# Expert numbers packed and read once, routed blocks written out, and 11 of 32 experts loaded beside the blocks

## The chip, the cores and the metric

The kernel runs on one core of a Trainium2 chip. The metric is the device time of the whole program in microseconds. The time before is 4682.44 us, the median of three runs (4677.71 to 4683.45).

## The reference

Two layers work on 1792 tokens (32 sequences of 56) with 256 features. Each has a cross attention and a feed-forward part, each behind a layer norm and added to its input. The change lies in the feed-forward part of layer 0, a mixture of 32 experts (M = 176) beside a shared expert of twice that width:

```python
scores = sigmoid(x @ gate_w)
# two groups of eight experts are masked out, six of the rest are selected
weights = original_scores[selected] / sum
xs = x_exp[argsort(selected)]             # 6 x 1792 rows, sorted by expert
g = ragged_dot(xs, w_gate, group_sizes)
u = ragged_dot(xs, w_up, group_sizes)
d = ragged_dot(silu(g) * u, w_down, group_sizes)
expert_out = sum(d[unsorted] * weights)
shared = silu(x @ sw_gate) * (x @ sw_up) @ sw_down
out = expert_out + shared
```

All of it is float32 in the reference. The kernel computes each such product as three float16 products (high x high, high x low, low x high), weights and rows being kept as a high and a low half.

## The kernel before

Six phases follow one another: queries, attention and mixing of layer 0, its experts, then queries and attention of layer 1, and the last feed-forward part. The phases named here are `mix0_phase` and `experts_phase`.

**The end of mix0_phase.** Routing gives every (token, choice) a row in a buffer in which each expert has a whole number of blocks of 256 rows, at least one; there are NBX = 74 blocks in all, sorted by expert. VectorE counts for each block which expert it belongs to (L1161 to L1163), TensorE turns the column into a row (L1218), and VectorE copies the 74 numbers as int32 into `g.be` (L1165). GpSimd had set the two words ahead of them to zero (L1030).

**experts_phase** has a queue of turns, one per block u. The blocks 0 to 13 are the shared expert, two halves for each of seven blocks of tokens; u = 14 to 87 are the 74 routed blocks. An `up` of a block is 18 matmuls (gate and up projection), a `down` 10; TensorE runs up(u) and then down(u - 2), so that ScalarE, VectorE and GpSimd have two blocks of time for the activation between them.

- SyncE (SP) loads the weights of an expert with five DMAs (`weights`, L1333 to L1337) into one of three staging buffers. During the shared turns it loads in each turn two experts and one tile of 112 token rows (`rows`, L1342). In a routed turn u it issues, in this order, the transposed load of the rows of block u + 2 (`load_x`, L1310, behind up(u)), the weights of an expert if there is one in this turn, and the store of block u - 2 (`store_y`, L1317, behind the copy of its result).
- ScalarE converts an expert's staged weights to the high halves in four operations (L1430 to L1434), and behind that computes the turn's silu (`gate_`, L1441) and the high half of the activation.
- VectorE makes the low halves of the weights in four operations (L1476 to L1483), then the turn's product (L1496) and the copy of the result of block u - 2 out of PSUM (L1518).
- GpSimd scatters the tiles of token rows into the sorted buffer, 96 indirect DMAs (L1392), six for each of 16 tiles, with four buffers for the tiles. Behind that it computes the low half of the activation in every routed turn (L1405).

The routed blocks begin when all 96 sends have landed, since SP waits for them ahead of the first two loads of x. Which experts are loaded in a turn says `experts_at`: 28 of them two by two in the turns 0 to 13, and four in the turns 14 to 17. The turns up to u = 19 and the last ones are written out on SP, ScalarE, VectorE and GpSimd, the rest is a loop over pairs of turns (`blocks`).

TensorE has an order of its own. `group` (L1588) reads ten expert numbers into its registers, eight for the blocks of the group and two more because `down` is two blocks behind, and then runs eight blocks with them. Four groups are written out (the blocks 0 to 31, which wait for the weights of expert t ahead of block t, L1594), five run in a loop, and the last group has two blocks. The numbers in the registers are added to the address of the weights in each matmul.

Of the kernel before, what the change touches and what calls it, by code (L numbers as in the profile page):

```python
# [32 lines left out]
NB = NBX + NBS  # L33
NU = NBX + 2 * NBS
LAG = 2
F = 1024
FB = F // 128
WS = 64.0
# [33 lines left out]
def later(tile, d):  # L72

    n, par, half = tile
    return n + d, (par + d) % 2, half + (par + d) // 2
# [842 lines left out]
def mix0_phase(nc, g, io):  # L918

    with phase(nc) as (ctx, a):  # L920
# [31 lines left out]
        jcol = a.sb("m_jcol", [128, 1])  # L952
        past = a.sb("m_past", [128, NE])
        bcol = a.sb("m_bcol", [128, 1])
        pY = a.ps("m_pY", [128, 512])
        pX = a.ps("m_pX", [128, 512])
        pL = a.ps("m_pL", [128, 512])
# [44 lines left out]
        @block.gpsimd  # L1002
        def _(pool):
            def rstd(t, k, _):
                pool.wait_ge(s["var"], t + 1)
                nc.gpsimd.tensor_tensor(rs[:], ve[:], g.mhalf[0:TT, 0:1], ALU.pow).then_inc(s["rstd"], 1)

            def rows(t, k, half):

                pool.wait_ge(s["xn_ready"], t + 1)  # L1010
                wait(pool, kept[k], 16 * half)
                passed(pool, p_gate)
                row = xn[:, k].rearrange("t (p c) -> t c p", c=KC)
                high, low = (xr[:, k, n].rearrange("t (c p) -> t c p", c=KC) for n in range(2))
                nc.gpsimd.tensor_copy(high, row).then_inc(s["rows"], 1)
                pool.wait_ge(s["rows"], 2 * t + 1)
                passed(pool, p_gate)
                nc.gpsimd.tensor_tensor(low, row, high, ALU.subtract).then_inc(s["rows"], 1)

            made = Counted(pool, s["made"])  # L1020
            made(nc.gpsimd.memset(ones[:], 1.0))
            made(nc.gpsimd.iota(jcol[:], [[0, 1]], base=0, channel_multiplier=1,
                                allow_small_or_imprecise_dtypes=True)).done()

            made(nc.gpsimd.affine_select(out=before[:], in_=ones[:], compare_op=ALU.is_ge, fill=0.0, base=-1,
                                         pattern=[[1, 128]], channel_multiplier=-1))
            for n in range(2):
                made(nc.gpsimd.affine_select(out=spread[:, n], in_=ones[0:NE, 0:NE], compare_op=ALU.is_ge, fill=0.0,
                                             base=n - 1, pattern=[[1, NE]], channel_multiplier=-1))
            made(nc.gpsimd.memset(g.be[:, 0:LAG], 0))  # L1030
            pipeline(pool, NT, [(rstd, 0), (rows, -1)])

        @block.scalar
# [23 lines left out]
        def _(dve):  # L1057
# [99 lines left out]
            own(nc.vector.tensor_copy(g.s6[:], s8[:, :, 0:TOPK]))  # L1157
            own(nc.vector.tensor_scalar(g.idx[:], s8[:, :, 0:TOPK], 1.0, None, ALU.subtract))

            dve.wait_ge(s["made"], 6)  # L1160
            own(nc.vector.tensor_scalar(past[:], pX[:, NE:2 * NE], jcol[:, 0:1], None, ALU.is_le)).done()  # L1161
            own(nc.vector.tensor_reduce(bcol[:], past[:], AX.X, ALU.add)).done()
            nc.vector.tensor_scalar(bcol[:], bcol[:], NE - 1.0, None, ALU.min).then_inc(s["listed"], 1)  # L1163
            dve.wait_ge(s["turned"], 1)
            nc.vector.tensor_copy(g.be[:, LAG:LAG + NBX], pY[0:1, 0:NBX]).then_inc(s["filled"], 1)  # L1165

        @block.tensor
        def _(pe):
# [52 lines left out]
def experts_phase(nc, g, io):  # L1221
# [4 lines left out]
    GB = 8  # L1226
    NSH = 2 * NBS
    STG = 3
    PER = 2
    FIRST = [NE, NE + 1]  # L1230
    LINE = FIRST + list(range(NE))
    AT = {e: n for n, e in enumerate(LINE)}
    LATE = NE - PER * NSH
    SENDS = [(t, k) for t in range(NT) for k in range(TOPK)]
    with phase(nc) as (ctx, a):
        stg = a.sb("d_stg", [128, STG, 2, KC, M])
# [34 lines left out]

        def blocks(eng, turn, high):

            for u in range(-high, NSH + 6):
                turn((u, u % 2, u // 2))
            pairs = (NU - high - NSH - 6) // 2
            with eng.Fori(0, pairs) as i:
                turn((2 * i + NSH + 6, 0, i + NSH // 2 + 3))
                turn((2 * i + NSH + 7, 1, i + NSH // 2 + 3))
            for u in range(NSH + 6 + 2 * pairs, NU + LAG):  # L1280
                turn((u, u % 2, u // 2))

        def main(e, n):
# [11 lines left out]
        def experts_at(u):  # L1295

            if not isinstance(u, int):
                return []
            if u == -1:
                return FIRST  # L1300
            if 0 <= u < NSH:
                return list(range(PER * u, PER * u + PER))
            return [PER * NSH + u - NSH] if NSH <= u < NSH + LATE else []

        def load_x(eng, gate, tile):
            v, vk, _ = tokens_of(tile)
# [231 lines left out]
        def _(pe):  # L1538
            def up(tile, e):
                u, k, _ = tile  # L1540
                _, vk, vhalf = tokens_of(tile)
                pe.wait_ge(x_in[vk], 16 * vhalf + 16)

                wait(pe, s["h_ready"], 2 * (u - 1))
                for n in range(3):
                    out = ps[k][n] if n < 2 else ps[k][n][0:64 + MT]
                    for c in range(KC):
                        last = three_products(nc, out, columns(e, 0, n, c), columns(e, 1, n, c), xb[:, vk, 0, c],
                                              xb[:, vk, 1, c], start=(c == 0), stop=(c == KC - 1))
                last.then_inc(s["up_done"], 1)  # L1550
# [19 lines left out]
            def down_shared(v):  # L1570
# [5 lines left out]
                        last = down_part(pd[v % 2][:, b], k, NE + k, slice(b * 128, (b + 1) * 128), k == 0, k == 1)  # L1576
                last.then_inc(s["down_done"], 2)

            pe.wait_ge(s["zeroed"], 2)
            pe.wait_ge(s["w_lo"], 8)  # L1580
            for u in range(NSH):
# [1 line left out]
                if u > LAG and u % 2:  # L1583
                    down_shared((u - LAG) // 2)

            def group(i, count):

                _, held = nc.values_load_multi_w_load_instructions(  # L1588
                    g.be[0:1, ds(GB * i, count + LAG)], [mybir.EngineType.PE], min_val=0, max_val=NX - 1)
                for n in range(count):  # L1590
                    tile = (GB * i + n + NSH, n % 2, GB // 2 * i + n // 2 + NSH // 2)
                    if isinstance(i, int) and GB * i + n < NE:

                        pe.wait_ge(s["w_lo"], 4 * AT[GB * i + n] + 4)  # L1594
                    up(tile, held[n + LAG])
                    if isinstance(i, int) and GB * i + n < LAG:
                        if n == LAG - 1:
                            down_shared(NBS - 1)
                    else:
                        down(later(tile, -LAG), held[n])  # L1600
                return held[count:]

            full = NBX // GB
            for i in range(NE // GB):
                group(i, GB)
            with pe.Fori(NE // GB, full) as i:
                group(i, GB)
            for n, e in enumerate(group(full, NBX - GB * full)):
                u = NU - LAG + n
                down((u, u % 2, u // 2), e)  # L1610

def q1_phase(nc, g, io):
# [923 lines left out]
def build(nc, io):  # L2537
    with ExitStack() as ctx:
# [16 lines left out]
        io.xs = nc.dram_tensor("scratch_xs", [TOK, H], F32, kind="Internal").ap()  # L2555
        with ExitStack() as inner:
            b = Alloc(nc, inner)
            g.be = b.sb("be", [1, LAG + NBX], I32)
            g.comb = b.sb("comb", [TT, NT, NE])
            g.slot = b.sb("slot", [TT, NT, NE])  # L2560
            g.s6 = b.sb("s6", [TT, NT, TOPK])
            mix0_phase(nc, g, io)
            g.wg = b.sb("wg", [128, NX, 2, 2, KC, 128], F16)
            g.wt = b.sb("wt", [128, NX, 2, KC, 64 + MT], F16)
            g.wd = b.sb("wd", [128, NX, 2, 2, H], F16)
            experts_phase(nc, g, io)
# [41 lines left out]
```

## Time and profile before

| | us |
|---|---|
| median of three runs | 4682.44 |
| lowest and highest run | 4677.71, 4683.45 |
| the profiled execution's own time | 4708.63 |
| its span in the trace | 4706.5 |
| TensorE (PE) busy | 3904.1 (83%) |
| VectorE (DVE) busy | 3443.8 (73%) |
| GpSimd (POOL) busy | 2778.1 (59%) |
| ScalarE (ACT) busy | 2449.9 (52%) |

The rows in this document come from one profiled execution. Times are microseconds from the start of the span; busy time is that of instructions that compute or send; register, branch and semaphore instructions and the issuing of DMAs by SP do not count as busy. In the rows, PEq and SPq are the sequencers of TensorE and SyncE, L12 is line 12 of the kernel, and `out<-in` names what an instruction writes and reads. A helper's matmuls carry the helper's lines (L111 to L113). A bracket at the end of a row is the idle time of the engine before it and what ended it; "issue" is time in which the engine waited for nothing that the profile shows. PEclk is the granted TensorE clock as a share of full speed. The experts phase lies between 2758 and 3216 us.

### The profile page before, as it was taken

The page shows a single profiled execution, that of the slowest core. Times are in us where ns is not written, and L with a number is a line of the kernel's source. Part 1 is how long each engine was busy: PE and PEld are TensorE (multiplying, and loading weights), DVE is VectorE, ACT ScalarE, POOL GpSimd, SP SyncE. Part 2 cuts the span into 40 slices and gives each one's busy share as a digit, 9 for nine tenths or more (in the row PEclk, how much of TensorE's full clock was granted, in tenths as well). Part 3 has the DMA queues.
Part 4 walks back from the last instruction along what each step waited for, and adds up shares of the span by engine and source line. Part 5 has one row for each costly group of instructions (what it writes and reads, how often), then busy time and mean ns, then how long its engine had stood idle before and what let it go on. Part 6 is the DMA issues. An engine that isn't in the chain of part 4 may idle for free. (4 is left out here: it accounts for less than half of the span.)

```text
span 4706.5 us, 104529 instructions
## 1 busy us (share of the span) xinstructions
PE 3904.1 (83%) x34578; PEld 2973.1 (63%) x34579; DVE 3443.8 (73%) x5403; ACT 2449.9 (52%) x4087; POOL 2778.1 (59%) x2145
## 2 busy tenths in 40 slices
PE   5669999999999999999999735883199999999945
PEld 3437777767767776777777724773167767677734
DVE  4657787877877777878877236445789888888957
ACT  4635555545545555555555114331157777777843
POOL 5577777767767776777773144335635555555632
PEclk8879999999999999999999967996599999999966
DMA  6357777767767677687774547554344444444410
GB/s 242 113 133 148 167 153 160 168 132 162 161 141 163 145 159 150 152 173 150 155 160 103 172 127 215 140 141 126 113 123 130 119 123 125 124 118 129 110 38 25
DMA packets 1236097, 657.45 MB, mean 140 GB/s; under 512 B 1087825, under 2 KB 1162449, under 8 KB 1230654
## 3 DMA queue, kind: packets, MB, share of 16 engines
q1 hardware_dynamic: 1218654, 606.60, 54.8%
q0 software_dynamic: 9216, 22.03, 1.6%
q10 hardware_dynamic: 7760, 22.55, 1.3%
q8 instruction: 298, 4.88, 0.4%
q14 instruction: 169, 1.38, 0.1%
HBM read 187.16 MB, written 142.34 MB: 70 GB/s over the span
## 5 line engine op out<-in xcount | busy, mean ns | idle before, releaser
L2007 POOL TENSOR_TENSOR b_pTl<-b_pe,b_pTh 125x1344 f16<-125x1344 f32 x192 | 538.4, 2804 | 482.8 <-ACT b_pTh L2066 458.4
L111 PE MATMUL a_pa<-a_pTh,a_ch 125*128 125x224 f16 x3072 | 796.5, 259 | 1.9 <-DMA a_pTl<-a_pl 1.9
L113 PE MATMUL a_pa<-a_pTh,a_cl 125*128 125x224 f16 x3072 | 795.5, 259 | 0.0
L112 PE MATMUL a_pa<-a_pTl,a_ch 125*128 125x224 f16 x3072 | 795.4, 259 | 0.0
L826 POOL TENSOR_TENSOR a_ksq<-a_kb 125x512 f32<-125x512 f32 x384 | 474.0, 1234 | 350.9 <-DVE a_kb L759 283.4
L698 ACT ACTIVATE a_pr<-a_pr,a_nmax 112x1500 f32<-112x1500 f32 x256 | 395.7, 1546 | 374.3 <-DVE a_nmax L777 374.2
L843 POOL TENSOR_TENSOR a_kb<-a_kb,a_rk 125x512 f32<-125x512 f32 x384 | 540.4, 1407 | 69.1 <-POOL a_kb L843 34.8
L791 DVE SCALAR_TENSOR_TENSOR a_pl<-a_pr,a_inv,a_ph 112x1500 f16<-112x1500 f32 x256 | 502.3, 1962 | 46.1 <-ACT a_ph L705 45.2
L705 ACT ACTIVATE a_ph<-a_pr,a_inv 112x1500 f16<-112x1500 f32 x256 | 395.5, 1545 | 222.1 <-DVE a_inv L786 222.1
L2112 DVE TENSOR_REDUCE b_mx<-b_ps 112x3 f32<-112x1500 f32 x256 | 439.0, 1715 | 95.3 <-PE b_ps L2189 93.9
L777 DVE CUSTOM_DVE_ANT_0 a_pr<-a_ps,a_mask 112x1500 f32<-112x1500 f32 x256 | 438.8, 1714 | 70.3 <-PE a_ps L113 65.3
L2059 ACT ACTIVATE b_pe<-b_pt 125x448 f32<-125x448 f32 x768 | 393.3, 541 | 163.2 <-PE b_pt L2211 157.8
L747 DVE TENSOR_REDUCE a_ssk<-a_ksq 125x8 f32<-125x1024 f32 x192 | 233.9, 1218 | 223.2 <-POOL a_ksq L826 222.5
L111 PE MATMUL a_pw<-a_wk,a_cT 128*128 128x512 f16 x768 | 304.3, 396 | 91.5 <-DVE a_kTl L765 42.7
L688 ACT ACTIVATE a_kTh<-a_pw 128x500 f16<-128x500 f32 x384 | 224.8, 585 | 251.1 <-PE a_pw L869 249.8
L2066 ACT ACTIVATE b_pTh<-b_pe 125x1344 f16<-125x1344 f32 x256 | 337.0, 1317 | 5.0 <-PE b_po L2227 1.8
L837 POOL TENSOR_TENSOR a_rk<-a_rk,mhalf 125x8 f32<-125x8 f32 x192 | 314.2, 1636 | 35.2 <-POOL a_rk L833 35.2
L112 PEld LDWEIGHTS a_pa<-a_pTl,a_ch 125*128 125x128 f16 x3072 | 301.0, 98 | 23.9 <-issue 0.3
L759 DVE SCALAR_TENSOR_TENSOR a_kb<-a_pw,a_bk 125x512 f32<-125x512 f32 x384 | 262.7, 684 | 70.0 <-PE a_pw L113 64.4
L111 PEld LDWEIGHTS a_pa<-a_pTh,a_ch 125*128 125x128 f16 x3072 | 300.3, 98 | 21.3 <-DVE a_al L797 2.1
L765 DVE TENSOR_TENSOR a_kTl<-a_pw,a_kTh 128x500 f16<-128x500 f32 x384 | 256.1, 673 | 69.3 <-ACT a_kTh L688 68.9
L111 PE MATMUL a_ps<-a_kTh,a_qh 128*112 128x500 f16 x768 | 294.3, 383 | 14.1 <-DVE a_nmax L777 13.2
(376 smaller groups left out, 10953.5 us busy)
## 6 DMA issues: line engine op xcount, KB each, us to landing
b_ks<-b_kn SPq DMA_DIRECT2D x768, 93.8 KB
scratch_cT<-a_cT SPq DMA_DIRECT2D x64, 768.0 KB
b_cT<-scratch_cT SPq DMA_DIRECT2D x32, 1536.0 KB
a_ctx<-ctx SPq DMA_DIRECT2D x128, 360.0 KB
scratch_xd<-q_zero ACTq DMA_DIRECT2D x4, 4736.0 KB
scratch_yd<-e_y SPq DMA_DIRECT2D x74, 256.0 KB
scratch_oT<-a_ot SPq DMA_DIRECT2D x16, 896.0 KB, 4.2
m_oT<-scratch_oT SPq DMA_DIRECT2D x16, 896.0 KB
```

What stands on the lines that cost most here:

```text
L111: nc.tensor.matmul(out, a_hi, b_hi, start=start, stop=False)
L112: nc.tensor.matmul(out, a_hi, b_lo, start=False, stop=False)
L113: return nc.tensor.matmul(out, a_lo, b_hi, start=False, stop=stop)
L698: nc.scalar.activation(pr[:, n % 2], pr[:, n % 2], ACT.Exp, scale=-1.0, bias=nmax[:, par, n:n + 1], accum_out=rsum[:, par, n:n + 1]).then_ ...
L705: nc.scalar.activation(ph[:, n % 2, :, 0:KP], pr[:, n % 2].rearrange("p (k c) -> p k c", c=KP), ACT.Copy, scale=inv[:, par, n:n + 1]).then ...
L777: nc.vector.tensor_tensor_reduce(out=pr[:, n % 2].rearrange("p (a k) -> p a k", k=500), in0=ps_s[0:RP, :, 0:500], in1=mask[:].rearrange("p ...
L791: nc.vector.scalar_tensor_tensor(pl[:, n % 2, :, 0:KP], pr[:, n % 2].rearrange("p (k c) -> p k c", c=KP), inv[:, par, n:n + 1], ph[:, n % ...
L826: nc.gpsimd.tensor_tensor(ksq[:, n % 4], kb[0:KP, n % KBN], kb[0:KP, n % KBN], ALU.mult).then_inc(s["k_squared"], 1)
L843: nc.gpsimd.tensor_tensor(k4, k4, rk[:, 1, NKV * t:NKV * t + NKV].unsqueeze(2) .to_broadcast([KP, NKV, HD]), ALU.mult).then_inc(s["k_norme ...
L2007: nc.gpsimd.tensor_tensor(pTl[:, n % 2, :, 0:RP], pe_[:, n % NP], pTh[:, n % 2, :, 0:RP], ALU.subtract).then_inc(s["l_pool"], 1)
L2059: nc.scalar.activation(pe_[:, r % NP, 4 * third:4 * third + 4], ps_t[at % 2][0:KP, 0:4 * RP].rearrange("p (k c) -> p k c", c=RP), ACT.Exp) ...
L2112: nc.vector.tensor_reduce(mx[:, par, n], ps_s[0:RP, :, 0:500], AX.X, ALU.max).then_inc(s["max_ready"], 1)
```

## The change

The 74 expert numbers are packed four to a word, as digits to the base 32, into 19 words. TensorE reads the 19 words into registers once, ahead of the shared blocks, and takes each number out of its word with a division and a remainder where it is first used. All 74 routed blocks are written out on TensorE; the groups and their loop are gone. 21 experts are loaded in the turns 0 to 13 (alternately one and two), and 11 in every second turn from 14 to 34. The turns up to u = 35 are written out on the other engines (`LONG` = 36). In `mix0_phase` VectorE multiplies the 76 entries by 1, 32, 1024 and 32768 and adds them by fours, two operations ahead of the copy; GpSimd makes the four factors in four memsets instead of one memset of `g.be`.

```diff
@@ -33,6 +33,8 @@
 NB = NBX + NBS
 NU = NBX + 2 * NBS
 LAG = 2
+PACK = 4
+NWORD = -(-NBX // PACK)
 F = 1024
 FB = F // 128
 WS = 64.0
@@ -952,6 +954,9 @@
         jcol = a.sb("m_jcol", [128, 1])
         past = a.sb("m_past", [128, NE])
         bcol = a.sb("m_bcol", [128, 1])
+        digit = a.sb("m_digit", [1, PACK])
+        digits = a.sb("m_digits", [1, NWORD, PACK])
+        word = a.sb("m_word", [1, NWORD])
         pY = a.ps("m_pY", [128, 512])
         pX = a.ps("m_pX", [128, 512])
         pL = a.ps("m_pL", [128, 512])
@@ -1027,7 +1032,8 @@
             for n in range(2):
                 made(nc.gpsimd.affine_select(out=spread[:, n], in_=ones[0:NE, 0:NE], compare_op=ALU.is_ge, fill=0.0,
                                              base=n - 1, pattern=[[1, NE]], channel_multiplier=-1))
-            made(nc.gpsimd.memset(g.be[:, 0:LAG], 0))
+            for n in range(PACK):
+                made(nc.gpsimd.memset(digit[:, n:n + 1], float(NE ** n)))
             pipeline(pool, NT, [(rstd, 0), (rows, -1)])
 
         @block.scalar
@@ -1157,12 +1163,15 @@
             own(nc.vector.tensor_copy(g.s6[:], s8[:, :, 0:TOPK]))
             own(nc.vector.tensor_scalar(g.idx[:], s8[:, :, 0:TOPK], 1.0, None, ALU.subtract))
 
-            dve.wait_ge(s["made"], 6)
+            dve.wait_ge(s["made"], 5 + PACK)
             own(nc.vector.tensor_scalar(past[:], pX[:, NE:2 * NE], jcol[:, 0:1], None, ALU.is_le)).done()
             own(nc.vector.tensor_reduce(bcol[:], past[:], AX.X, ALU.add)).done()
             nc.vector.tensor_scalar(bcol[:], bcol[:], NE - 1.0, None, ALU.min).then_inc(s["listed"], 1)
             dve.wait_ge(s["turned"], 1)
-            nc.vector.tensor_copy(g.be[:, LAG:LAG + NBX], pY[0:1, 0:NBX]).then_inc(s["filled"], 1)
+            own(nc.vector.tensor_tensor(digits[:], pY[0:1, 0:NWORD * PACK].rearrange("a (w n) -> a w n", n=PACK),
+                                        digit[:].unsqueeze(1).to_broadcast([1, NWORD, PACK]), ALU.mult)).done()
+            own(nc.vector.tensor_reduce(word[:], digits[:], AX.X, ALU.add)).done()
+            nc.vector.tensor_copy(g.be[:], word[:]).then_inc(s["filled"], 1)
 
         @block.tensor
         def _(pe):
@@ -1226,11 +1235,11 @@
     GB = 8
     NSH = 2 * NBS
     STG = 3
-    PER = 2
+    EARLY = 21
+    LONG = NSH + 2 * (NE - EARLY)
     FIRST = [NE, NE + 1]
     LINE = FIRST + list(range(NE))
     AT = {e: n for n, e in enumerate(LINE)}
-    LATE = NE - PER * NSH
     SENDS = [(t, k) for t in range(NT) for k in range(TOPK)]
     with phase(nc) as (ctx, a):
         stg = a.sb("d_stg", [128, STG, 2, KC, M])
@@ -1271,13 +1280,13 @@
 
         def blocks(eng, turn, high):
 
-            for u in range(-high, NSH + 6):
+            for u in range(-high, LONG):
                 turn((u, u % 2, u // 2))
-            pairs = (NU - high - NSH - 6) // 2
+            pairs = (NU - high - LONG) // 2
             with eng.Fori(0, pairs) as i:
-                turn((2 * i + NSH + 6, 0, i + NSH // 2 + 3))
-                turn((2 * i + NSH + 7, 1, i + NSH // 2 + 3))
-            for u in range(NSH + 6 + 2 * pairs, NU + LAG):
+                turn((2 * i + LONG, 0, i + LONG // 2))
+                turn((2 * i + LONG + 1, 1, i + LONG // 2))
+            for u in range(LONG + 2 * pairs, NU + LAG):
                 turn((u, u % 2, u // 2))
 
         def main(e, n):
@@ -1299,8 +1308,9 @@
             if u == -1:
                 return FIRST
             if 0 <= u < NSH:
-                return list(range(PER * u, PER * u + PER))
-            return [PER * NSH + u - NSH] if NSH <= u < NSH + LATE else []
+                return list(range(EARLY * u // NSH, EARLY * (u + 1) // NSH))
+            n = EARLY + (u - NSH) // 2
+            return [n] if u >= NSH and u % 2 == 0 and n < NE else []
 
         def load_x(eng, gate, tile):
             v, vk, _ = tokens_of(tile)
@@ -1576,6 +1586,8 @@
                         last = down_part(pd[v % 2][:, b], k, NE + k, slice(b * 128, (b + 1) * 128), k == 0, k == 1)
                 last.then_inc(s["down_done"], 2)
 
+            _, words = nc.values_load_multi_w_load_instructions(
+                g.be[0:1, 0:NWORD], [mybir.EngineType.PE], min_val=0, max_val=NE ** PACK - 1)
             pe.wait_ge(s["zeroed"], 2)
             pe.wait_ge(s["w_lo"], 8)
             for u in range(NSH):
@@ -1583,31 +1595,28 @@
                 if u > LAG and u % 2:
                     down_shared((u - LAG) // 2)
 
-            def group(i, count):
-
-                _, held = nc.values_load_multi_w_load_instructions(
-                    g.be[0:1, ds(GB * i, count + LAG)], [mybir.EngineType.PE], min_val=0, max_val=NX - 1)
-                for n in range(count):
-                    tile = (GB * i + n + NSH, n % 2, GB // 2 * i + n // 2 + NSH // 2)
-                    if isinstance(i, int) and GB * i + n < NE:
-
-                        pe.wait_ge(s["w_lo"], 4 * AT[GB * i + n] + 4)
-                    up(tile, held[n + LAG])
-                    if isinstance(i, int) and GB * i + n < LAG:
-                        if n == LAG - 1:
-                            down_shared(NBS - 1)
-                    else:
-                        down(later(tile, -LAG), held[n])
-                return held[count:]
-
-            full = NBX // GB
-            for i in range(NE // GB):
-                group(i, GB)
-            with pe.Fori(NE // GB, full) as i:
-                group(i, GB)
-            for n, e in enumerate(group(full, NBX - GB * full)):
-                u = NU - LAG + n
-                down((u, u % 2, u // 2), e)
+            experts = {}
+
+            def expert(t):
+
+                if t not in experts:
+                    word = words[t // PACK]
+                    experts[t] = (word // NE ** (t % PACK)) % NE
+                return experts[t]
+
+            for t in range(NBX):
+                tile = (t + NSH, t % 2, (t + NSH) // 2)
+                if t < NE:
+
+                    pe.wait_ge(s["w_lo"], 4 * AT[t] + 4)
+                up(tile, expert(t))
+                if t >= LAG:
+                    down(later(tile, -LAG), expert(t - LAG))
+                elif t == LAG - 1:
+                    down_shared(NBS - 1)
+            for t in range(NBX - LAG, NBX):
+                u = t + NSH
+                down((u, u % 2, u // 2), expert(t))
 
 
 def q1_phase(nc, g, io):
@@ -2555,7 +2564,7 @@
         io.xs = nc.dram_tensor("scratch_xs", [TOK, H], F32, kind="Internal").ap()
         with ExitStack() as inner:
             b = Alloc(nc, inner)
-            g.be = b.sb("be", [1, LAG + NBX], I32)
+            g.be = b.sb("be", [1, NWORD], I32)
             g.comb = b.sb("comb", [TT, NT, NE])
             g.slot = b.sb("slot", [TT, NT, NE])
             g.s6 = b.sb("s6", [TT, NT, TOPK])
```

## Rows read from the trace of the kernel before

**Rows 1.** Windows: three stretches; busy us (x instructions) by engine, PEclk, DMA share, GB/s
```profile
2758.00:2920.00 162.00, 66.27 (x373) 47.90 (x372) 82.56 (x187) 59.19 (x154) 100.52 (x99) 0.66 0.76 210
2920.00:3018.00 98.00, 77.65 (x615) 66.05 (x616) 44.26 (x93) 38.82 (x92) 27.96 (x42) 0.90 0.57 139
3018.00:3216.00 198.00, 172.04 (x1479) 151.67 (x1476) 82.81 (x161) 72.91 (x158) 70.84 (x107) 0.95 0.57 140
```

**Rows 2.** Waits of POOL, 2764 to 2916 us: us in total, times, longest
```profile
POOL scratch_xd L1392 <- issue: 27.1, 89, 0.3
POOL scratch_xd L1392 <- DMA d_xr<-scratch_xd: 26.1, 6, 12.5
```

**Rows 3.** Tile d_xr: duration in ns min/median/max, first and last start
```profile
L1392 POOL DMA_INDIRECT scratch_xd<-d_xr,idx x96: 937/942/1412, 2764.0 to 2912.6; - x96
```

**Rows 4.** Timeline of SP: weights of early experts at two paces
```profile
2801.87 0.70 SPq L1333 DMA_DIRECT2D d_stg<-L_ffn_w_gate  x1
2803.27 0.70 SPq L1333 DMA_DIRECT2D d_stg<-L_ffn_w_up  x1
...
2824.87 0.43 SPq L1333 DMA_DIRECT2D d_stg<-L_ffn_w_gate  x1
...
2832.17 0.47 SPq L1333 DMA_DIRECT2D d_stg<-L_ffn_w_gate  x1
```

**Rows 5.** Timeline of PE: first matmuls of u = 14, 16, 34, 36, and of later blocks
```profile
2920.06 0.28 PE L111 MATMUL e_pab<-e_xb,wg 128*128 128x256 f16 x1 [1.24 <-DMA e_xb<-scratch_xd]
...
2931.53 0.28 PE L111 MATMUL e_pab<-e_xb,wg 128*128 128x256 f16 x1 [0.71 <-DVE e_h L1499]
...
3011.99 0.27 PE L111 MATMUL e_pab<-e_xb,wg 128*128 128x256 f16 x1
...
3018.12 0.27 PE L111 MATMUL e_pab<-e_xb,wg 128*128 128x256 f16 x1
...
3087.62 0.39 PE L111 MATMUL e_pab<-e_xb,wg 128*128 128x256 f16 x1 [4.01 <-issue]
...
3093.33 0.27 PE L111 MATMUL e_pab<-e_xb,wg 128*128 128x256 f16 x1
...
3111.71 0.27 PE L111 MATMUL e_pab<-e_xb,wg 128*128 128x256 f16 x1
...
3208.14 0.27 PE L111 MATMUL e_pab<-e_xb,wg 128*128 128x256 f16 x1
```

**Rows 6.** Waits of PE, 3018 to 3216 us: us in total, times, longest
```profile
PE e_pab L111 <- issue: 21.7, 7, 4.0
```

**Rows 7.** Line L1588: duration in ns min/median/max, first and last start
```profile
L1588 PEldq FUSED_REGOPS  x94: 146/146/165, 2917.0 to 3204.6; - x94
...
L1588 PEldq TENSOR_LOAD <-be x10: 350/1430/1587, 2915.6 to 3203.3; - x10
```

**Rows 8.** Timeline of PE: the first matmul of the shared expert
```profile
2773.57 0.37 PE L111 MATMUL e_pab<-e_xb,wg 128*128 128x256 f16 x1 [15.40 <-DVE wt L1480]
```

**Rows 9.** Timeline of SP: a turn with late weights and the one behind it
```profile
2943.93 1.29 SPq L1310 DMA_TRANSPOSE e_xb<-scratch_xd  x1
...
2953.49 0.41 SPq L1317 DMA_DIRECT2D scratch_yd<-e_y  x1
2954.01 1.41 SPq L1310 DMA_TRANSPOSE e_xb<-scratch_xd  x1
2955.53 1.14 SPq L1317 DMA_DIRECT2D scratch_yd<-e_y  x1
2956.90 1.28 SPq L1310 DMA_TRANSPOSE e_xb<-scratch_xd  x1
```

**Rows 10.** Timeline of ACT: the conversion of late weights
```profile
2949.59 0.63 ACT L1430 ACTIVATE wg<-d_stg 128x512 f16<-128x512 f32 x1 [6.33 <-DMA d_std<-L_ffn_w_down]
```

**Rows 11.** Timeline of DVE: a small operation at the end of mix0_phase
```profile
2757.59 0.15 DVE L1163 TENSOR_SCALAR m_bcol<-m_bcol 128x1 f32<-128x1 f32 x1
```

**Rows 12.** DMA queues, 2920 to 3080 us: packets, MB, share of 16 engines
```profile
q8 instruction: 12, 0.20, 0.5%
```

## The prediction

> **What bounds the kernel now.** The change touches the experts phase alone, and the windows view cuts it in three [rows 1]. From 2758 to 2920 us TensorE computes the shared expert while POOL scatters the token rows; PE is busy 66.27 of 162 us, POOL 100.52. From 2920 to 3018 us (blocks u = 14 to 35) PE is busy 77.65 of 98 us, and from 3018 to 3216 us 172.04 of 198. So POOL comes close to its bound in the first stretch, TensorE in the third.
>
> *First stretch.* No routed block may be loaded before the last of 96 sends. POOL's waits show 26.1 us in six waits for token rows, the longest 12.5; the rest is 0.3 us of issue per send [rows 2], and a send itself is 0.94 us, the first at 2764.0, the last at 2912.6 [rows 3]. So 96 x (0.942 + 0.30) = 119 us is the floor, and 119 + 26.1 nearly fills the 148.6 us. The token rows are fetched by SP, behind the weights of the early experts. SP's queue shows two paces [rows 4]: at 2801.87 us its issues are 1.40 us apart, at 2824.87 a whole turn (two experts, one tile of rows) takes 7.30 us to the next. POOL needs 6 x 1.242 = 7.45 us a tile. At the second pace SP keeps up with POOL; only the first pace starves it.
>
> *Third stretch.* A block takes (3111.71 - 3093.33) / 6 = 3.063 us [rows 5]. From u = 36 (3018.12) to u = 87 (3208.14) are 51 blocks: 190.02 us, while 51 x 3.063 = 156.2. The excess of 33.8 us is the breaks at which PE reads the next ten expert numbers: 21.7 us of it is PE's idle time put down to issue, seven times and up to 4.0 us [rows 6]; the remainder is late operands and, behind most breaks, a block at the lower granted clock level (1.2 GHz): the first matmul takes 0.39 us at 3087.62, 0.27 in the steady block [rows 5].
>
> *Second stretch.* Four of its turns load an expert beside the block; the chain of one of these prices the late loads below.
>
> **Against which time.** The profiled execution took 4708.63 us (span 4706.5, 2.1 around it), 26.2 above the median of 4682.44. That is almost the 26.1 us of row waits, and the slow pace of SP stands nowhere else in the trace. I take it that the profiled execution has these waits and the timed runs do not: a choice, whose opposite is rival 1. The sum is a difference, worked on this execution's rows and put onto the median. A measurement of this kernel can tell 0.2% (9.4 us) from no change.
>
> **The parts and their costs.**
>
> *Breaks removed.* A read is one TENSOR_LOAD of 1.43 us and ten register operations of 0.146 [rows 7], 2.9 us, in line with the idle times. After the change, 19 words are read ahead of the shared expert, where PE waits until 2773.57 for the first weights (15.4 us, [rows 8]); by the same rows that is at most 2 x 1.43 + 19 x 0.146 = 5.6 us, hidden. Unhidden it would be 5.6 us. The third stretch gains between 21.7 us (idle alone, clock still lost) and 33.8 (all excess). I take 33, since the steady block's 0.27 us shows what follows when nothing breaks it. Breaks in the second stretch go too, but there the late loads decide.
>
> *Decoding a number.* New work on PE's sequencer: a division and a remainder per block, not in the trace. The nearest row is 0.146 us each, 0.29 a block. PE's sequencer runs ahead of the array, which has work without a gap in the steady block, so I cost it at nothing; with no cover it is 74 x 0.29 = 21.5 us (rival 3). A gain is excluded, since only work is added.
>
> *Late loads.* 11 experts instead of 4 are loaded at u = 14, 16, ... 34. Expert n is first needed by block n, 21 blocks after its load for the first of them and 11 for the last, so no block waits for its own weights, and the staging buffer that a load reuses was converted turns before. What waits is the queue. In the late turn that I follow, SP issues the load of x at 2943.93, then five weight DMAs, and the next load of x only at 2954.01: 10.08 us [rows 9]. Between, ACT has sat 6.33 us until the weights had landed, with the gate of the current block behind them in its order [rows 10]; DVE's product and, behind it, the copy of the older block wait for that gate, SP's store (2953.49) for the copy, and the next load of x is queued behind the store. PE waits for that x. The ordinary turn behind it takes 2956.90 - 2954.01 = 2.89 us [rows 9]. A pair is 12.97 us. 1.14 - 0.41 = 0.73 us of it may be that turn's slow store issue, so the lower bound is 12.2. Before, u = 14 to 16 took 2931.53 - 2920.06 = 11.47 [rows 5]; with ten more pairs, u = 36 is reached after 11.47 + 122 = 133.5 to 11.47 + 129.7 = 141.2 us. It is 98.06 now [rows 5]. The loss is 35.4 to 43.1; I take the middle, 39.3, since one pair gives no reason for either end.
>
> *First stretch.* Seven experts fewer are loaded there: 35 DMA issues, 28 ACT and 28 DVE operations. Without starvation POOL's floor of 119 us stays, so the gain is 0 to 3 us (the ends of the tiles' fetches); I take 1.
>
> *End of the mixing phase.* DVE multiplies and reduces before the copy of the numbers, two small operations more on the serial path; one such takes 0.15 us [rows 11], so 0.3 bare to 0.7 with waits. I take 0.5. The memsets on POOL (nine instead of six) are made long before and cost nothing; bare, three of about 0.1 us.
>
> *Sum:* 39.3 - 33 - 1 + 0.5 = +5.8 us, thus 4682.4 + 5.8 = 4688.2, say **4688**. By its bounds: 35.4 - 33.8 - 3 + 0.3 = -1 to 43.1 - 21.7 + 0.7 = +22, where both upper ends together are unlikely: 4681 to 4698.
>
> **A rule that speaks against it.** The queue of instruction fetches moved 12 packets between 2920 and 3080 us, most of it written-out blocks [rows 12]; the steady written-out blocks there took (3018.12 - 3011.99) / 2 = 3.07 us [rows 5], no more than the loop's 3.063. The traced blocks say that it is hidden, and the sum goes by that.
>
> **Rivals.**
>
> 1. *The scatter is starved in the timed runs too.* For it: the waits are there, POOL's only ones of size. Against it: the coincidence of 26.2 and 26.1, and PE too starts instructions late in those stretches. With 35 of 140 issues gone, 20 to 26 of 26.1 us go, say 23: 4688 - 23 = 4665 (4660 to 4668). Chance 0.38.
>
> 2. *Written-out code stalls TensorE* (slower). The place is the 40 former loop blocks, 123 us at 3.063. At 12 fetches in 160 us about 10 more come there, up to 20 with 36 instead of 20 turns written out on the other engines. One that drains PE is priced by the nearest wait for a DMA, 1.24 us at 2920.06 [rows 5]: 12 to 25 us, say 20, thus 4708. It decides where PE's sequencer has no more than that in its queue. Against it stands the 3.07. Chance 0.10.
>
> 3. *The decoding does not hide*, or the words are not held in registers, so that the change does not do what it says: +21.5 us, 4709. Chance 0.06.
>
> **The numbers.** My forecast has 0.46: 0.02 of it faster by over 0.2%, 0.36 within, 0.08 slower. Rival 1: 0.37 faster, 0.01 within. Rivals 2 and 3: 0.16 slower. So faster 0.39, same 0.37, slower 0.24. Signs are mixed; the forecast's own range is 4681 to 4698. The range of 8 in 10 reaches down to rival 1's far end, 4660, and up to 4698, leaving out rivals 2 and 3 and the forecast's tails.
>
> **What would show it.** In the changed profile: no TENSOR_LOAD between blocks, no idle time put down to issue in the third stretch, u = 36 to 87 in about 157 us, late turns of 10 us from load to load with ACT waiting some 6 us for weights, 130 to 141 us from the first routed block to u = 36, and hardly any waits for rows on POOL. If POOL's first-to-last send falls from 148.6 us to about 122 and the timed median falls by 15 us or more, rival 1 holds. If late turns come out at 7 us or less, the price of the late loads was wrong; if blocks take more than 3.1 us, rival 2 or 3.

## The result, and the profile after it

The changed kernel takes 4708.01 us (median of five, 4700.23 to 4716.82), the kernel before 4683.16 (five runs, 4677.71 to 4686.72). The ratio is 1.0059, with a 95% interval of 1.0048 to 1.0070: about 25 us slower. The forecast was 4688 with a range up to 4698.

The stages are cut here as the prediction cut them, by the first matmul of a block on TensorE. In the changed kernel (timeline of PE; the helper's lines are now L113 to L115) the first matmuls of u = 14, 16, 18 and 36, of a block in between, and of u = 87 are these:

```profile
2896.07 0.39 PE L113 MATMUL e_pab<-e_xb,wg 128*128 128x256 f16 x1 [21.57 <-issue]
...
2910.10 0.39 PE L113 MATMUL e_pab<-e_xb,wg 128*128 128x256 f16 x1 [5.67 <-DVE e_h L1509]
...
2923.37 0.39 PE L113 MATMUL e_pab<-e_xb,wg 128*128 128x256 f16 x1 [5.10 <-DVE e_h L1509]
...
3045.50 0.39 PE L113 MATMUL e_pab<-e_xb,wg 128*128 128x256 f16 x1 [4.78 <-DVE e_h L1509]
...
3074.10 0.28 PE L113 MATMUL e_pab<-e_xb,wg 128*128 128x256 f16 x1 [1.21 <-issue]
...
3212.55 0.27 PE L113 MATMUL e_pab<-e_xb,wg 128*128 128x256 f16 x1
```

Against [rows 5]: u = 14 comes 24 us earlier than in the profiled execution of before; u = 14 to 36 takes 149.4 us instead of 98.1; u = 36 to 87 takes 167.05 instead of 190.02. A pair of late turns is (3045.50 - 2910.10) / 10 = 13.54 us.

The waits of PE from 2896 to 3045 us, and then from 3046 to 3211 us (us in total, times, longest), say who holds it up. The first answers to no row of before; the second stands against [rows 6].

```profile
PE e_pab L113 <- DVE e_h L1509: 50.4, 10, 5.8
```

```profile
PE e_pab L113 <- DMA e_xb<-scratch_xd: 5.2, 5, 1.1
PE e_pab L113 <- issue: 1.4, 2, 1.2
```

So the breaks of 21.7 us are gone, as planned, and seven small waits have come in their place, most of them put down to the rows x. In the late turns PE waits ten times some 5 us for VectorE's product. That product waits for ScalarE, whose waits from 2900 to 3045 us are:

```profile
ACT wg L1440 <- DMA d_std<-L_ffn_w_down: 105.0, 11, 25.7
ACT e_hh L1460 <- DVE e_h L1509: 15.1, 20, 1.0
```

ScalarE stands 105 us in front of late weights, once for each of the 11 experts. In one of these turns (u = 24) the wait passes from engine to engine like this, until PE starts block u = 26:

```profile
2974.34 0.63 ACT L1440 ACTIVATE wg<-d_stg 128x512 f16<-128x512 f32 x1 [7.83 <-DMA d_std<-L_ffn_w_down]
...
2975.74 0.36 ACT L1451 ACTIVATE e_h<-e_pab 128x256 f32<-128x256 f32 x1
...
2977.00 0.43 DVE L1509 SCALAR_TENSOR_TENSOR e_h<-e_pc,e_h 48x256 f32<-48x256 f32 x1
...
2977.73 0.39 PE L113 MATMUL e_pab<-e_xb,wg 128*128 128x256 f16 x1 [5.04 <-DVE e_h L1509]
```

The same turn and the one behind it in SP's queue, against [rows 9]:

```profile
2968.45 1.23 SPq L1320 DMA_TRANSPOSE e_xb<-scratch_xd  x1
...
2971.77 0.42 SPq L1347 DMA_DIRECT2D d_std<-L_ffn_w_down  x1
2978.24 0.41 SPq L1327 DMA_DIRECT2D scratch_yd<-e_y  x1
2978.76 1.42 SPq L1320 DMA_TRANSPOSE e_xb<-scratch_xd  x1
2980.29 1.01 SPq L1327 DMA_DIRECT2D scratch_yd<-e_y  x1
2981.85 1.23 SPq L1320 DMA_TRANSPOSE e_xb<-scratch_xd  x1
```

It is 10.31 us from load to load (10.08 before) and 3.09 for the ordinary turn behind it (2.89 before). The windows view gives the clock, against [rows 1]:

```profile
2760.00:2896.00 136.00, 58.82 (x373) 46.27 (x372) 78.05 (x175) 52.88 (x135) 99.12 (x99) 0.70 0.80 221
2896.00:3045.00 149.00, 92.83 (x616) 75.22 (x616) 47.86 (x105) 42.70 (x106) 26.70 (x40) 0.75 0.49 117
3045.00:3220.00 175.00, 165.93 (x1476) 147.53 (x1476) 83.38 (x162) 74.19 (x160) 72.15 (x108) 0.98 0.69 160
```

PEclk falls to 0.75 in the late turns (0.90 in the middle stretch before) and rises to 0.98 behind them (0.95 before). The first matmuls of the late pairs take 0.39 us against 0.27 in a steady block: after some 5 us without work for PE, every pair begins at the lower level, 1.2 GHz.

The words are read once, by one load and 19 register operations, ahead of 2769.2 us, while PE has nothing to do yet (line L1589: ns min/median/max, first and last start):

```profile
L1589 PEldq FUSED_REGOPS  x19: 146/146/165, 2763.8 to 2769.0; - x19
...
L1589 PEldq TENSOR_LOAD <-be x1: 2037/2037/2037, 2761.7 to 2761.7; - x1
```

And POOL hardly waits for rows any more; its waits from 2766 to 2890 us, against [rows 2]:

```profile
POOL scratch_xd L1402 <- issue: 28.7, 94, 0.3
POOL scratch_xd L1402 <- DMA d_xr<-scratch_xd: 0.6, 1, 0.6
```

Whether that is a gain is the first question, since the time rose all the same.

### The profile page after: what moved, and what is told of

The parts are those of the page before. It is cut to its first block and busy times, and to the rows that moved or that the text cites. A ratio compares the mean times of both kernels' runs of the same rounds, so it can differ in the third digit from the quotient of the medians.

```text
span 4715.1 us, 104029 instructions
## 1 busy us (share of the span) xinstructions
PE 3910.4 (83%) x34578; PEld 2979.1 (63%) x34578; DVE 3445.6 (73%) x5405; ACT 2450.4 (52%) x4087; POOL 2777.2 (59%) x2148
## 5 line engine op out<-in xcount | busy, mean ns | idle before, releaser
L113 PE MATMUL a_pa<-a_pTh,a_ch 125*128 125x224 f16 x3072 | 796.8, 259 | 1.9 <-DMA a_pTl<-a_pl 1.9
L115 PE MATMUL a_pa<-a_pTh,a_cl 125*128 125x224 f16 x3072 | 795.7, 259 | 0.0
L113 PE MATMUL a_pw<-a_wk,a_cT 128*128 128x512 f16 x768 | 305.2, 397 | 90.9 <-DVE a_kTl L767 42.8
L113 PEld LDWEIGHTS a_pa<-a_pTh,a_ch 125*128 125x128 f16 x3072 | 300.3, 98 | 21.4 <-DVE a_al L799 2.1
L113 PE MATMUL a_ps<-a_kTh,a_qh 128*112 128x500 f16 x768 | 294.0, 383 | 14.1 <-DVE a_nmax L779 13.2
```

Source lines behind the costliest of these rows:

```text
L113: nc.tensor.matmul(out, a_hi, b_hi, start=start, stop=False)
L115: return nc.tensor.matmul(out, a_lo, b_hi, start=False, stop=stop)
```

## The experiments

**Stages of all runs.** Each is the difference of two first matmuls in the run's own trace, as above. "Shared" is from the first matmul of the shared expert to u = 14. The times of the first two rows are those of one profiled execution, the others are medians.

| run | shared | u = 14 to 36 | u = 36 to 87 | time, us | ratio to before (95%) |
|---|---|---|---|---|---|
| before (profiled) | 146.5 | 98.1 | 190.0 | 4708.63 | |
| e1 before again | 123.4 | 101.0 | 190.0 | 4683.01 | |
| changed | 120.6 | 149.4 | 167.1 | 4708.01 | 1.0059 (1.0048 to 1.0070) |
| e2 code alone | 123.5 | 96.4 | 167.0 | 4663.80 | 0.9954 (0.9937 to 0.9970) |
| e3 loads alone | 121.8 | 149.4 | 191.6 | 4730.31 | 1.0096 (1.0078 to 1.0115) |
| e4 convert later | 120.4 | 80.9 | 168.8 | 4643.01 | 0.9901 (0.9882 to 0.9921) |
| e5 three buffers | 122.9 | 92.5 | 156.2 | 4647.36 | 0.9932 (0.9916 to 0.9949) |
| e6 more code | 122.9 | 96.1 | 165.9 | 4648.39 | 0.9933 (0.9918 to 0.9949) |
| e7 later and three | 121.3 | 75.8 | 156.4 | 4621.01 | 0.9877 (0.9861 to 0.9892) |
| e8 the same, 28 early | 124.5 | 71.9 | 156.2 | 4621.99 | 0.9873 (0.9857 to 0.9890) |

The times of e1 to e4 stand beside a before of 4687.83 us, those of e5 to e8 beside 4680.57. The whole times of one kernel differ by 10 us and more between executions, while its stages in two traces agree to about 3 us (the shared stretch of that first profile apart); so mechanisms are read from the stages and verdicts from the ratios.

**e1: the kernel before, profiled a second time.** No edit.

> The kernel before, unchanged, looked at once more. Theory (the waits for token rows belong to the one profiled execution, not to the timed runs): the time is near 4683 us and POOL's waits for rows come to under 5 us, the last send about 120 us behind the first. Rival (the scatter of before is starved in all its runs, and the change cured that): 20 us or more of waits for rows again, at a time near 4683.

The time was 4683.01 us in this profiled execution. The scatter (tile d_xr) and POOL's waits between 2758 and 2885 us:

```profile
L1392 POOL DMA_INDIRECT scratch_xd<-d_xr,idx x96: 937/942/1405, 2758.4 to 2884.5; - x96
```

```profile
POOL scratch_xd L1392 <- issue: 28.6, 94, 0.3
POOL scratch_xd L1392 <- DMA d_xr<-scratch_xd: 0.5, 1, 0.5
```

0.5 us of waits for rows instead of 26.1, and 126.1 us from the first send to the last instead of 148.6. The slow pace of SP's queue in [rows 4] is not there either. In the other 12 traces these waits come to 0.9 us at most. So the 26 us were one execution's, and the changed kernel has cured nothing that the timed runs had. It was not SP alone that was slow in it. The windows view shows 15 us in which PE ran 10 matmuls, and VectorE and ScalarE were busy for half a microsecond each:

```profile
2857.00:2872.00 15.00, 3.79 (x10) 1.24 (x9) 0.46 (x1) 0.51 (x1) 8.46 (x9) 0.52 0.47 153
```

POOL's longest wait for rows, 12.5 us, ends just behind it (2880.55). Between two matmuls into the same tile, where no other engine is waited for, PE stood still for a quarter of a microsecond or more 15 times in this experts phase (nine of them in these 15 us), and never in that of the other 13 traces. What slowed the engines in that one execution stays open. From here on e1 is the trace of before that the changed one is compared with: u = 14 to 36 is 101.0 us in it.

```profile
2891.10 0.39 PE L111 MATMUL e_pab<-e_xb,wg 128*128 128x256 f16 x1 [12.92 <-DMA e_xb<-scratch_xd]
...
2992.11 0.27 PE L111 MATMUL e_pab<-e_xb,wg 128*128 128x256 f16 x1
...
3182.14 0.27 PE L111 MATMUL e_pab<-e_xb,wg 128*128 128x256 f16 x1
```

**e2: the TensorE code alone**, with the loads of before.

```diff
-    EARLY = 21
-    LONG = NSH + 2 * (NE - EARLY)
+    EARLY = 28
+    LONG = NSH + 6
...
-            n = EARLY + (u - NSH) // 2
-            return [n] if u >= NSH and u % 2 == 0 and n < NE else []
+            return [EARLY + u - NSH] if NSH <= u < NSH + NE - EARLY else []
```

> The changed TensorE code (words read once, all blocks written out) with the load schedule of before: 28 experts early, four in the turns 14 to 17. Theory: the stretch from u = 36 to 87 takes the 167 us of the changed kernel instead of 190, and two breaks more go between u = 17 and 36, worth some 7 us: 23 to 30 us faster than before, 4653 to 4660. Rival (written-out code costs more in the timed runs than the trace shows, so that it is the code that made the changed kernel slower): no faster than before.

The time was 4663.80 us, 24.0 below its before, with an interval of 14 to 30: the low end of the 23 to 30 expected. (The time itself is above the 4653 to 4660 expected, as the before beside it is 4.7 us above the first one.) The stretch from u = 36 took 167.0 us, as in the changed kernel, and the four late turns and two breaks ahead of it 4.6 us less than in e1. The code is a gain, not the loss.

**e3: the loads alone**, in the kernel before.

```diff
...
-            for u in range(-high, NSH + 6):
+            for u in range(-high, LONG):
...
-                return list(range(PER * u, PER * u + PER))
-            return [PER * NSH + u - NSH] if NSH <= u < NSH + LATE else []
+                return list(range(EARLY * u // NSH, EARLY * (u + 1) // NSH))
+            n = EARLY + (u - NSH) // 2
+            return [n] if u >= NSH and u % 2 == 0 and n < NE else []
```

> The load schedule of the change (21 early, 11 in every second turn from 14 to 34) with the TensorE code of before, groups and loop. Theory: the late turns cost 149.4 - 98.1 = 51 us, less about 7 for two breaks that lie inside them: 44 to 51 us slower, 4727 to 4734. Rival (scatter starved in every run of before): 24 us less than that, 4703 to 4710.

The time was 4730.31 us, 42.5 above its before (37 to 54 by the interval). The late turns took 149.4 us, the same as with the new code: the two breaks that lie in them cost nothing there, because PE waits for the activation anyway. The two halves nearly add up: 42.5 - 24.0 = +18.5 against +24.9 for the whole. Of the rest, 4.6 us are the two breaks, which e2 gains and the whole does not; what is left lies within the intervals.

**e4: the conversion two turns later.** In the changed kernel, ScalarE and VectorE convert a late expert's weights behind the activation of the turn u + 2; loads and counts stay.

```diff
-                for e in experts_at(tile[0]):
-                    high_weights(e)
+                u = tile[0]
+                if isinstance(u, int) and u < NSH:
+                    for e in experts_at(u):
+                        high_weights(e)
                 if exists(tile, NU):
                     gate_(tile)
                     high(tile)
-                u = tile[0]
+                if isinstance(u, int) and u >= NSH + 2:
+                    for e in experts_at(u - 2):
+                        high_weights(e)
```

(VectorE's `low_weights` likewise, and LONG is two more.)

> The changed kernel, but ScalarE and VectorE convert a late expert's weights two turns after its loads, behind that turn's own activation. Theory (the price of a late load is the activation queued behind the wait for weights): a pair of turns falls from 13.5 us to 6.2 to 8, bounded by SP's 4.1 us in a turn with loads, so 149 us become 70 to 90: 60 to 79 us off the changed kernel's 4708, 4629 to 4648. Rival (what costs is the transfer itself, or SP's queue of five more DMAs ahead of the store): pairs stay above 11 us and the time above 4680.

The time was 4643.01 us, and u = 14 to 36 fell from 149.4 to 80.9:

```profile
2892.98 0.39 PE L113 MATMUL e_pab<-e_xb,wg 128*128 128x256 f16 x1 [20.54 <-issue]
...
2973.84 0.27 PE L113 MATMUL e_pab<-e_xb,wg 128*128 128x256 f16 x1
```

The same five DMAs go out in the same turns of SP. ScalarE's waits from 2900 to 2974 us hold no weights any more:

```profile
ACT e_h L1451 <- PE e_pc L115: 15.2, 13, 1.9
ACT e_hh L1460 <- DVE e_h L1513: 13.6, 19, 1.6
```

So neither the transfer nor the issue of late weights costs much: 22 steady blocks are 22 x 3.063 = 67.4 us, and of the 82 us above that 13.5 are left. The rest was the order on ScalarE and VectorE (the run moves the conversion on both and does not tell them apart), in which the current block's activation stands behind a wait that nobody is in a hurry for.

**e5: a third buffer for the rows x**, on e2. The load is issued three blocks ahead instead of two, and SP's turns are all written out, since the buffer goes by u modulo 3.

```diff
-        xb = a.sb("e_xb", [128, 2, 2, KC, TC], F16)
+        xb = a.sb("e_xb", [128, 3, 2, KC, TC], F16)
...
-                if exists(later(tile, 2), NU):
-                    load_x(sp, gate, later(tile, 2))
+                if exists(later(tile, 3), NU):
+                    load_x(sp, gate, later(tile, 3))
```

It is aimed at the waits left between u = 36 and 87, seven in the changed kernel and eight in e2:

```profile
PE e_pab L113 <- DMA e_xb<-scratch_xd: 7.5, 7, 1.3
PE e_pab L113 <- issue: 1.3, 1, 1.3
```

This is the one at 3074.10 in the changed kernel, in SP's queue, and the instruction queue from 3071.4 to 3072.8 us:

```profile
3069.02 1.23 SPq L1320 DMA_TRANSPOSE e_xb<-scratch_xd  x1
3071.14 0.38 SPq L1327 DMA_DIRECT2D scratch_yd<-e_y  x1
3072.00 1.84 SPq L1320 DMA_TRANSPOSE e_xb<-scratch_xd  x1
```

```profile
q8 instruction: 1, 0.02, 5.2%
```

The load for that block was issued at 3069.02; a fetch of instructions fell on its end, and the next load took 1.84 us to issue instead of 1.23. Each of the six largest waits of the stretch has a fetch that starts 2.4 to 2.7 us ahead of PE's restart; one between 3082.4 and 3083.9 us cost nothing. That the rows were late can be read from the semaphore events of the trace, which count the landing of a load in 16 parts. Of the load at 3069.02, 15 parts had landed after 3.26 us and the last after 4.79. The last part came 4.6 to 4.9 us after the issue in exactly the six loads ahead of the six waits, and after 3.1 to 4.1 us in all others of the stretch. In e2 the seven waits of 1.0 to 1.3 us follow, in the same way, the seven loads that took 4.7 to 4.9 us.

> The kernel of the run with the code alone (28 early, changed TensorE code) with a third buffer for the rows x of a block, so that SP loads three blocks ahead; SP's turns are all written out for it. Theory (the gaps of 1.1 to 1.5 us that are left between u = 36 and 87 are rows that land late, because an instruction fetch of 16 KB falls on the end of their load): the gaps go, 167 us become 157 to 158, and the time falls by 8 to 10 us to about 4655. Rival (PE itself waits for its instructions): seven or eight such gaps stay, 166 us or more, no gain.

The time was 4647.36 us, and the stretch took 156.2 us, 51 x 3.063 to the last tenth, with as many fetches (15 in the queue), and the windows view has PE busy all through and the full clock:

```profile
2989.80:3146.00 156.20, 156.20 (x1431) 142.42 (x1429) 78.77 (x154) 70.89 (x153) 68.18 (x102) 1.00 0.75 171
```

PE does not wait for its instructions here; late rows were the whole excess of e2. Single loads still land late (one 4.76 us after its issue), and nobody waits for them. That SP's turns are written out as well is not what helped: they are in e6 too, which keeps its waits.

**e6: more written-out code**, on e2: the other engines' loops are written out as well.

```diff
-    LONG = NSH + 6
+    LONG = NU - 4
```

> The kernel of the run with the code alone, with all turns written out on the other engines too, so that their code has to be fetched as well and nothing else changes. Theory (a fetch costs about 1.2 us where it falls on the end of a load of x, which some half of them did): 14 fetches between u = 36 and 87 become 20 or more, three to six gaps more, 4 to 8 us slower, 171 to 175 us for the stretch. Rival (only TensorE's own fetches cost): 167 us again.

The stretch took 165.9 us, so the rival's 167 is right and the theory's 171 to 175 wrong: there were 21 fetches, as expected, and 7.8 us of waits against 8.8 in e2. What the run does not tell is whether more fetches like those of q8 would cost more. The DMA queues from 2980 to 3144 us show that q8 moved as much as in the changed kernel, and that the six fetches added are of another queue and half the size:

```profile
q8 instruction: 15, 0.25, 0.7%
q14 instruction: 6, 0.05, 0.1%
```

**e7 and e8: both mends together**, e4's order and e5's third buffer; e8 with EARLY = 28, so with four late experts.

> The changed kernel (21 early) with the conversions two turns later and the third buffer for x. Theory: the late turns lose their last gaps of 1.2 to 2.1 us too, since SP's longer turns now only eat into one more block of distance: u = 14 to 36 falls from 80.9 to 69 to 73 us, u = 36 to 87 from 168.8 to 157 or 158, 20 us below the run with later conversions: 4618 to 4626. Rival (SP's 4.1 us in a turn with loads bound the pair): 80 us again for the first part, 4632.

> As the run before it, with 28 experts early and four in the turns 14, 16, 18 and 20. Theory (in the timed runs the scatter alone sets the first stretch, so that seven early experts more or less cost nothing, and late loads cost nothing once they are out of the way): within 4 us of the run with 21 early. Rival (seven more experts delay the first stretch): the first routed block starts 10 us or more later behind the last send or behind the start of the sends, and the time is as much higher.

They took 4621.01 and 4621.99 us, the fastest of all: 1.2% below the kernel before. The stretch from u = 36 is at its bound in both (156.4 and 156.2 us). From 14 to 36 e7 took 75.8 us, more than the 69 to 73 expected and less than the rival's 80: gaps of 0.2 to 1.9 us are left in the late turns, and no run shows what ends most of them. e8 has four such turns and took 71.9, but 3.3 us more ahead of u = 14. 21 or 28 early makes no difference to the time.

**e9 to e12: four kernels on one chip**, since e6 had come out as fast as e5 with 13 us more in its experts phase.

> The changed kernel once more, beside the three that follow. Expected from the stages of its first trace: 20 to 28 us slower than before; u = 14 to 36 in 149 us, u = 36 to 87 in 167.

> The run with the code alone again, on the chip of its neighbours, since the run with more code came out 0.2% lower against before on another chip, while its experts phase took only 2 us less (385.0 against 386.8). Theory (the difference lies ahead of the experts phase and is scatter between executions): within 5 us of the run with more code that follows. Rival (code written out on the other engines helps): 8 us or more above it.

> The run with three buffers again. Theory: the phase's 13 to 15 us (371.6 against 385.0 and 386.8) stand in the whole time too, 10 to 16 us below the run with the code alone. Rival (they are given back outside the phase): within 4 us of it, as the last call had it against the run with more code.

> The run with more code again. Theory: the time of the run with the code alone within 5 us, and a stretch u = 36 to 87 of 165 to 168 us. Rival (code written out on the other engines helps): 8 us or more below it.

Against a before of 4682.33 us these took 4711.12 (ratio 1.0064, interval 1.0047 to 1.0081), 4663.25, 4642.24 and 4652.47 us. The change is confirmed; the code alone gains 19.1 us here (24.0 above). The third buffer is worth 21.0 us, more than the 10 to 16 expected and the 15.7 that the experts phase shows (385.1 and 369.4 us from the first matmul of the shared expert to u = 87). The run with more code again came out 10.8 us below the one without, as its rival has it, with 1.2 us less in the experts phase (383.9); what it gains elsewhere in the program stays open. Of the 7.3 us between the two profiled executions, 5.8 lie behind u = 87, where both have the same code.

## Why the prediction was wrong

Each term had the sign that was forecast, and the choice against rival 1 was right. Two terms of the sum were mis-sized, both to the bad side: behind the first stands a wait that was read wrongly, behind the second a delay that was put at nothing. Compared with e1:

| term | forecast | measured | how |
|---|---|---|---|
| late loads | +39.3 (35.4 to 43.1) | +48.4 | 149.4 - 101.0 |
| breaks removed | -33 (-33.8 to -21.7) | -23.0 | 190.0 - 167.05 |
| first stretch | -1 (-3 to 0) | -2.8 | 123.4 - 120.6 |
| sum with 0.5 for the mixing phase | +5.8 | +23.1 | |

+23.1 is close to the +24.9 of the medians. The late loads lie outside their range, the breaks inside theirs, near the bad end; that end had been left out of the forecast's 4698, since both upper ends together were held to be unlikely.

*Late loads.* The step that failed is "A pair is 12.97 us", of which 12.2 was made the lower bound and the middle was taken. The pair measured 13.54 us, above both. The wait behind it had been read as "PE waits for that x", the x that is queued behind the store. It was another, and the row of u = 16 in [rows 5] names it already: the x of block u = 26 had been issued at 2968.45, and PE began that block at 2977.73, when VectorE's product of block 24 was done, since `up` writes the buffer in PSUM that this product empties. So the pair runs from `up` of a late turn over SP's load of x and the five loads behind it, their landing, ScalarE's conversion and gate, and the product, to `up` of the next late turn. The stores are not on this path, and the slow store issue of 0.73 us never was: in [rows 9] too the load behind it waits for `up` of the same block. But `up` is on it, and it runs at the lower level in each pair, after PE has idled some 5 us: 4.0 us in block 24 (2964.34 to 2968.36), against 2.1 in block 25. The turn of [rows 9] was no model for this: it is the last of four late turns in a row, and its load of x (2943.93) follows a store (2943.41) and not `up`. The first two blocks, priced at 11.47 from the one execution, took 14.03 in the changed kernel, beginning at the lower level too (0.39 us at 2896.07). ACT's wait (7.8 us where some 6 were named) and the product behind it are the mechanism that was forecast; e4 shows the cause by taking it away.

*Breaks.* The step that failed is "I take 33, since the steady block's 0.27 us shows what follows when nothing breaks it". Something did: 167.05 - 51 x 3.063 = 10.8 us. Of these, 2.4 belong to the late loads: block 36, behind the last of their waits, begins at the lower level and takes 5.49 us. The other 8.4 are the small waits. The steady written-out blocks of [rows 5] were an interval without a wait, and the prediction read from it that fetching is hidden. Rival 2 had the right source and a nearly right price (1.24 us each, the six largest seen at 0.9 to 1.2), but named the wrong victim: not PE's supply of instructions, but the loads of x, which have little time to spare with two buffers. The late landings and e5 settle that. By the prediction's own sign (more than 3.1 us a block; 167.05 / 51 = 3.28) this part of rival 2 came true. That its 4708 us is the time measured is luck: it had 20 us for the fetches, and 8.4 were found; the late loads make up the difference. The Trainium skill (Advanced Engine Details and Errata, ISA Cache) gives TensorE 128 KB for code, in lines of 16 KB. The trace agrees with the lines: 15 fetches moved 0.25 MB for 51 written-out blocks, and none ran during the loop of before (3080 to 3210 us). What a fetch costs, the traces had to say.

*Rival 1* was priced at -23 and given 0.38. e1 and e3 refute it: the loads alone cost 42.5 us, where it would have left some 20.

*Rival 3* fell: the decoding hides, and blocks without a wait run at 3.063 us.

*Mixing phase and reading of the words.* The two operations added in the mixing phase take 0.5 us, as forecast (from 2760.05 to 2760.56 on VectorE). The words were in registers by 2769.2 us, 6 us ahead of PE's first matmul: the reading took 7.5 us instead of at most 5.6, and hid.

## What to carry to other kernels

A load "beside" the work is cheap only if the conversion of what it brings is queued where its data has landed: put it behind the current block's steps on every engine that it passes. And follow the wait of the engine that bounds the stage to what its code really waits for, here a buffer in PSUM and not the rows. Where the loads of a loop have little time to spare, written-out code can bring waits for data instead of waits for code; one more buffer removed them here. And a single profiled execution that is 0.5% above the median is not to be summed with until a second profile has shown which of its waits are the kernel's.

## What the runs showed that was not expected

An instruction fetch of 16 KB can delay the last of the 16 parts of another queue's transposed load by 1.5 us (3069.02 in the changed kernel). There, from u = 36, the six fetches that started 2.3 to 2.5 us behind the issue of a load cost PE 0.9 to 1.2 us each, and the other nine at most 0.15. The start alone does not decide it: in e2 a fetch 2.47 us behind a load cost nothing, and one 2.60 us behind cost 1.0. In one execution of the kernel before PE, VectorE, ScalarE and SP's queue were slow to start instructions (most plainly from 2857 to 2872 us), and with them the scatter; in none of the later traces were they. No run here says by what.
